# Two rounds of a half head's attention-values product, put side by side in the order of work

## The reference, cut to what matters

```python
x = x + 0.5 * ffn(layernorm(x))
x = x + attention(layernorm(x))
x = x + 0.5 * ffn(layernorm(x))
```

```python
scores = jnp.einsum('bhqd,bhkd->bhqk', q, k) * scaling
attn = jax.nn.softmax(scores, axis=-1)
out = jnp.einsum('bhqk,bhkd->bhqd', attn, v)
```

## Time and profile before

| what | value |
|---|---|
| runs of the kernel | 1638.84, 1641.56, 1642.37 us |
| the profiled execution: span from first to last instruction | 1642.9 us |
| PE busy | 1575.7 us, 96% of the span, 8356 matmuls |
| DVE, ACT, POOL busy | 869.0, 656.8 and 896.1 us (53%, 40%, 55%) |
| the heads, from the first scores to the last round of values | 617.4 to 1095 us |

### The profile page before, as it was taken

The page is one execution under the profiler, slowest core; times in us unless marked ns, Lnnn a source line. Parts: engine busy times, 40 slices in busy tenths (PEclk is TensorE's granted clock), DMA queues, the critical chain, the costliest instruction groups (busy, mean ns, idle before and its releaser), DMA issues.

```text
span 1642.9 us, 24109 instructions
## 1 busy us (share of the span) xinstructions
PE 1575.7 (96%) x8356; PEld 1143.5 (70%) x8356; DVE 869.0 (53%) x1482; ACT 656.8 (40%) x974; POOL 896.1 (55%) x745
## 2 busy tenths in 40 slices
PE   6999999999998899999999999999999999999996
PEld 5778899999886774444444444347778799889984
DVE  5554322222278686787777777667563422222235
ACT  4422232322232316666666666654431222222310
POOL 3107476405666857877888788511306195333735
PEclk9999999999998998999999999999999999999998
DMA  9306455324272321112112120123106264333337
GB/s 342 130 1 245 174 186 186 133 78 154 91 247 81 90 71 44 31 39 39 31 39 40 29 43 17 25 50 132 57 1 214 110 235 140 132 132 132 132 98 235
DMA packets 89344, 180.15 MB, mean 110 GB/s; under 512 B 30224, under 2 KB 31120, under 8 KB 86928
## 3 DMA queue, kind: packets, MB, share of 16 engines
q1 hardware_dynamic: 76400, 104.95, 21.2%
q0 software_dynamic: 12832, 73.67, 12.6%
HBM read 106.48 MB, written 55.97 MB: 99 GB/s over the span
## 4 chain that ended last, share of the span: by engine, by line
PE 72%; DMA 9%; DVE 8%; POOL 3%; ACT 3%; issue 3%; SPq 3%; POOLq 0%; DVEq 0%; ACTq 0%
PE PS L1187 10%; PE PS L1189 9%; PE PS L1188 9%; PE PS L1420 7%; PE PS L1434 6%; PE PS L1401 6%; PE PS L1450 3%; DMA xn<-x_routed 3%; DMA xs<-x_routed 3%; PE PS L1324 2%; PE PS L1329 2%; PE PS L1327 2%; PE PS L1326 2%; PE PS L1328 2%; PE PS L1325 2%
## 5 line engine op out<-in xcount | busy, mean ns | idle before, releaser
L1673 ACT ACTIVATE PT<-PS 128x1024 f32<-128x1024 f32 x256 | 258.2, 1024 | 127.7 <-PE PS L1420 126.5
L1970 DVE TENSOR_REDUCE nmf_later<-PS 128x1 f32<-128x1024 f32 x160 | 194.0, 1219 | 58.0 <-PE PS L1401 57.8
L1434 PE MATMUL PS<-PT,V 128*32 128x512 f32 x1024 | 203.7, 608 | 0.0
L2038 POOL TENSOR_TENSOR W<-raw,W 128x544 fp32r<-128x544 f32 x144 | 190.1, 1354 | 1.5
L1420 PE MATMUL PS<-QS,KS 98*128 98x512 f32 x512 | 179.2, 434 | 4.5 <-DVE nmf_first L1970 2.3
L979 POOL TENSOR_TENSOR added<-PT 128x1024 f32<-128x1024 f32 x56 | 136.4, 2436 | 76.9 <-ACT PT L1673 76.9
L1420 PEld LDWEIGHTS PS<-QS,KS 98*128 98x128 f32 x512 | 85.5, 191 | 130.7 <-issue 50.6
L1401 PE MATMUL PS<-KS,QS 96*128 96x512 f32 x512 | 168.9, 412 | 3.6 <-DVE nmf_first L1970 1.6
L1937 DVE TENSOR_TENSOR thid<-thid,PS 128x352 f32<-128x352 f32 x78 | 40.6, 521 | 245.8 <-ACT thid L1604 245.8
L2026 POOL DMA_DIRECT2D raw<-ffn_w x18 | 10.0, 555 | 249.7 <-POOLq L2024 194.0
L1187 PE MATMUL PS<-xh,W 128*128 128x512 f32 x352 | 141.0, 401 | 4.9 <-DVE hid L1848 2.2
(11 more groups left out here) (197 smaller groups left out, 3846.4 us busy)
## 6 DMA issues: line engine op xcount, KB each, us to landing
raw<-ffn_w POOLq DMA_DIRECT2D x18, 2176.0 KB, 10.3
y_routed<-ytile SPq DMA_DIRECT2D x78, 256.0 KB, 2.1
xn<-x_routed SPq DMA_DIRECT2D x40, 256.0 KB, 3.2
x_routed<-xq SPq DMA_DIRECT2D x1, 9984.0 KB, 29.4
xs<-x_routed SPq DMA_DIRECT2D x38, 256.0 KB, 3.4
QS<-later_hi SPq DMA_DIRECT2D x112, 64.0 KB, 2.0
raw<-ffn_w SPq DMA_DIRECT2D x6, 768.0 KB, 6.1
raw<-ffn_w SPq DMA_DIRECT2D x16, 272.0 KB, 4.2
```

Source lines behind the costliest of these rows:

```text
L1434: e.matmul(PS[i * QUARTER:(i + 1) * QUARTER, ob, :], V[:, b * QT + kt, g, :], PT[:, u % PTBUF, kt % 2 * GRP:(kt % 2 + 1) * GRP], start=rou ...
L1673: e.activation(PT[:, u % PTBUF, :], PS[:, i:i + 2, :].rearrange("p b n -> p (b n)"), ACT.Exp, scale=SCALE).then_inc(p_ready.sem, 1)
L1970: e.tensor_reduce(row_maxima(n)[:, h, t:t + 1], PS[:, i:i + 2, :].rearrange("p b n -> p (b n)"), AX.X, ALU.max, negate=True).then_inc(max_ ...
L2038: low = e.tensor_tensor(W[:, slot, 1, cs], raw[slot][:, cs], W[:, slot, 0, cs], ALU.subtract)
```

## The change

The item `("values", hh, 1)` is moved from step 1 to step 0 of the following half head, right behind `("values", hh, 0)`. Before, it stood behind the "row_max" and the "invert" of step 1. The items for the last of the 64 half heads, which stand after the loop, are not touched.

```diff
@@ -439,7 +439,7 @@
         if hh >= 0 and pair == 0:
-            work.extend([("sum", hh), ("values", hh, 0)])
+            work.extend([("sum", hh), ("values", hh, 0), ("values", hh, 1)])
             if maxima and un % QT == QT // 2:
@@ -447,8 +447,6 @@
         if hh >= 1 and pair == 1:
             work.append(("invert", hh - 1))
-        if hh >= 0 and pair == 1:
-            work.append(("values", hh, 1))
         if hh >= 0 and pair == 2:
```

## The result

The changed kernel is slower: 1655.35 us, median of 4 runs (1651.92 to 1657.50), against 1641.59 us for the kernel before. The medians are 13.8 us apart. The ratio is 1.0101, with a 95% interval from 1.0078 to 1.0124, that is 16.6 us, from 12.8 to 20.4. The prediction was 16 us. The profiled execution after took 1657.50 us and its span is 1655.7 us, so 1.8 us lie outside the span.

A forecast was written before the change was run, and what follows sets the result against it. PE's instruction order was taken as the bound in groups 0 to 6. +16.0 us from 55 half heads, +1 for the inversion and -1 for the last group gave +16 on 1641.6: 1657.6 us, range 1648 to 1668.

The forecast's parts named there:

- The bound: Groups 0 to 6: PE's instruction order is the time, PE being busy for 407.97 of 411 us.
- The gain: PE's switches between scores blocks and values rounds: 0.34 us saved per half head, 21.4 us over 63, if nothing waits.
- The new wait: Step 2's scores wait 0.53 us for DVE's step 0 reduction, restart 0.10 slower; net +0.29 us in 55 half heads, +16.0.
- What else the move touches: Other bank handovers, exponentials, POOL's additions and DMA order: no further wait or gain expected.
- the crossing point: DVE's step 0 reduction ready 1.76 us after that row_max block starts, restart included, would make the change cost nothing.
- the first rival: Switches win and no wait for DVE appears in the half heads: minus 21.4 us, 1620 us; chance 0.07.
- The inversion: DVE's wait for the sums' DMA, coming later relative to the third values round: from -2 to +6, taken as +1 us.
- The last group: No row_max, two pairs of banks: saved switches against DVE's additions, from -2.7 to +1, taken as -1 us.
- The sum: Whole kernel: +16 us on the median of 1641.6, giving 1657.6 us.
- The rivals: Four alternatives: switches win 1620 us (0.07), inversion becomes the bound 1670 (0.08), clock falls 1682 (0.04), no effect 1642 (0.04).
- The falling clock: Waits in the half heads make PE's granted clock fall in one of four: 24 us more, 1682 us; chance 0.04.

The follow-up runs named there:

- the first: Kernel before the change, with the second values round moved behind the first in the last group alone; ratio 0.9995 against the kernel before.
- fourth: Changed kernel with the half head's first row_max block put ahead of the two joined values rounds; ratio 1.0135 against the kernel before.
- tenth experiment: Changed kernel with DVE's inversion moved from step 1 to step 2, behind that step's row_max reduction; ratio 1.0080 against the kernel before.
- the eighth experiment: Kernel before the change, with DVE's inversion moved from step 1 to step 2, behind that step's row_max reduction; ratio 0.9991 against the kernel before.
- the fifth experiment: Changed kernel leaving out half of step 0's row_max reduction and half of step 1's exponential in the half heads; ratio 0.9988 against the kernel before.

## Why the prediction was right, point by point

- **The bound.** Right: PE's order of instructions was the time in groups 0 to 6, and each change of one half head's length is found again in the total (54 x 0.29 = 15.7 of 16.75 us).
- **The gain.** Right: V0 and V1 1.86 us (1.85 predicted), R1 without a switch. The kernel with both readers shortened shows 0.25 of the 0.34 us bare; the rest is S2's slower restart. The Trainium skill's sentence that a change of tiling mode drains TensorE ("TensorEngine Tiling (Array Packing)", Key Properties) agrees with the rows at 0.1 us for each of the two ends of a round. By itself it would have given the wrong sign.
- **The new wait.** Right in place, engine and size: S2 2.04 us behind R0's start (2.05), S2 itself 0.57 (0.57), one half head 7.61 to 7.66 (7.64). It is shown by the timeline, by its absence when the reduction is short, and by the last group, which has no "row_max" and did not lose.
- **What else the move touches.** In one place the wording was weaker than the facts. "R2 waits for the exponential of S1: free" is true only because S2 waits. R2 would reach those banks 0.33 us too early, and the prediction did not say that this second wait lay hidden behind the first; the crossing point given for the first rival (DVE ready 1.76 us behind R0's start) is wrong for the same reason. With DVE ready at 1.5 the kernel still took 7.42, because R2 could not start before the exponential of S1 was done, 2.31 us behind R0's start. So no faster reduction alone would have brought this order under 7.35, and the prediction's 7 in 100 for the switches winning stood partly on a condition that could not do it. A term was missing that the prediction had not counted: bank 7. The transpose of queries (L1381) needs it, and `store_head`'s multiplication, which frees it, comes later. The half heads with L1965, which are those with that transpose ahead of them, grew by 0.4 and not 0.29, about 1.4 us in all. In them the transpose starts 0.65 us behind R3 after the change and 0.54 before it, in nearly every one. The row of the weight load there (L1379 after) has 0.47 us of idle time, named for DVE, where 0.35 is the usual.
- **The inversion.** +1 us was taken, from -2 to +6. The long half heads have 3.9 us of extras after and had 4.9 before, by the distances of V2: -1. The two kernels with the inversion moved put its part at +2 instead, so its sign stays open; both lie within the range.
- **The last group.** -1 us was taken, and the eight distances show -1.0 in the kernel that moves only there and -1.8 after. The other -1.9 us of the profile are the border: about -1.6 are the clock's (below) and -0.3 the move's.
- **The sum.** +16 us against 13.8 by the medians and 16.6 by the ratio, 12.9 in the profiled heads. Groups 0 to 6 gave 16.75 where 17 were summed, and that it is so near is partly luck: the missing 1.4 us of bank 7 and an inversion that gave -1 by the distances instead of +1 nearly cancel. In the profiles the border's clock and the last group take the rest back; which part of that the medians hold stays open. Setting the span on the median was loose too: the executions after took 1.8 us more than their spans.
- **The rivals.** The falling clock did not come: granted 1.00 from 628 to 1052 us with a wait of 0.54 us in each half head. The mechanism of the Trainium skill's page "TensorE: Matmul & The Clock Gate", section "A second HAM failure mode: psum-queue depth-cycling", is therefore not met by pauses of this size here.

## What to carry to other kernels

Work that stands between a buffer's fill and its next use is cover, even if it is put there for no such reason. Before a block is moved to save a switch, count for each buffer that rotates the time from the writer's start to the next taker's start without that block, and hold it against the reader's latency (here 0.76 + 1.22 + 0.05 us for DVE and 0.66 + 1.02 + 0.05 for ACT, against 1.4 to 1.5 us of three blocks). Do it for every kind of reader in the row, also for the waits that the first one hides: removing one of two that overlap brings only the difference.

## What the runs showed of the hardware

- A matmul block that had to wait costs 0.1 us more than its wait, as much as behind a switch of the array's form (0.66 against 0.56 before a round, 0.57 against 0.47 before another block), whether DVE or ACT was waited for.
- At the border to the last group S0 waits in every profile for the reduction of the R3 right before it, since only two pairs of banks are left, about 1.4 us. In 4 of 12 profiles (before, the first, fourth and tenth experiment) the granted clock then went to one half, 1.2 GHz, for 3.4 us and the border took 8.8 to 9.1 us. In the others it stayed at 2.4 GHz and took 7.1 to 7.5. S0 and the round behind it before, with the fall, and in the eighth experiment, without:

```profile
1042.73 0.73 PE L1420 MATMUL PS<-QS,KS 98*128 98x512 f32 x2 [1.32 <-DVE nmf_later L1970]
1043.39 0.93 PE L1434 MATMUL PS<-PT,V 128*32 128x512 f32 x3
...
1052.97 0.73 PE L1420 MATMUL PS<-QS,KS 98*128 98x512 f32 x2 [1.32 <-DVE nmf_later L1970]
1053.63 0.63 PE L1434 MATMUL PS<-PT,V 128*32 128x512 f32 x3
```

  PE did the same ahead of it in both: it was busy for all of the 5 us up to V2, and then waited equally long. Where V0 and V1 stand together in the last group the border is 7.14 to 7.18 us without a fall and 8.78 to 8.81 with one; where they don't, it is 7.48 and 7.51 without and 9.07 with one. So a fall is about 1.6 us of a profile that no difference in the instructions explains, and the move is 0.3 us there.
- Shorter pauses did not bring it: 55 pauses of 0.54 us, one in each 7.64 us, brought no fall in the changed kernel's profile. A single one of 2.25 us did in the fifth experiment: granted 0.76 over 14 us.
